# The third expert layer computed for two of its three experts: batches sorted, gathered and scattered by indirect DMA

## Reference

```python
gate_scores = jax.nn.softmax(router_input @ gate_w + gate_b, axis=-1)
top_val, top_idx = jax.lax.top_k(gate_scores, TOP_K)                  # 3 experts, top 2
top_val = top_val / (jnp.sum(top_val, axis=-1, keepdims=True) + 1e-08)
pre = jnp.einsum('bsd,edf->ebsf', h, w1) + b1[:, None, None, :]
act = jnp.stack([jnp.tanh(pre[0]), jax.nn.gelu(pre[1], approximate=False), jax.nn.silu(pre[2])])
expert_out = jnp.einsum('ebsf,efd->ebsd', act, w2) + b2[:, None, None, :]
for i in range(TOP_K):
    j = top_idx[:, 0, i]                                              # by the batch's first row
    moe_out = moe_out + top_val[..., i:i + 1] * expert_out[j, batch_idx]
```

## Time and profile before

| | |
|---|---|
| median of 3 runs | 845.54 us (844.17 to 845.92) |
| profiled execution, its own time | 845.61 us |
| its span, first to last instruction | 843.5 us |
| mean granted clock of PE | 0.988 of full |
| layers 0 and 1 | 0 to 203.2 us of the span |
| layer 2 | 203.2 to 533.2 us |
| layer 3 | 533.2 to 843.5 us |

### The profile page before, as it was taken

The page is one execution under the profiler, slowest core; times in us unless marked ns, Lnnn a source line. Parts: engine busy times, 40 slices in busy tenths (PEclk is TensorE's granted clock), DMA queues, the critical chain, the costliest instruction groups (busy, mean ns, idle before and its releaser), DMA issues.

```text
span 843.5 us, 11203 instructions
## 1 busy us (share of the span) xinstructions
PE 821.4 (97%) x3981; PEld 669.1 (79%) x3981; DVE 385.0 (46%) x850; ACT 289.4 (34%) x541; POOL 247.4 (29%) x272
## 2 busy tenths in 40 slices
PE   4999999998999999999999999999999999999998
PEld 3488777776788888888888888778878888887886
DVE  2567777777322532252225222755454254336522
ACT  5344444444322232233223322234315323432520
POOL 3476677675343210021002100577200220021000
PEclk9699999999999999999999999999999999999999
DMA  8346446432330130013003200433040004002001
GB/s 260 62 114 167 153 155 201 143 131 83 100 100 26 50 111 3 1 62 100 0 0 104 57 0 0 150 99 89 26 137 0 25 14 122 0 25 99 1 1 51
DMA packets 53957, 63.72 MB, mean 76 GB/s; under 512 B 29153, under 2 KB 29409, under 8 KB 53658
## 3 DMA queue, kind: packets, MB, share of 16 engines
q1 hardware_dynamic: 49522, 48.70, 19.7%
q0 software_dynamic: 3888, 14.16, 5.3%
q10 hardware_dynamic: 512, 0.41, 0.2%
HBM read 44.36 MB, written 13.40 MB: 68 GB/s over the span
## 4 chain that ended last, share of the span: by engine, by line
PE 93%; DVE 3%; ACT 1%; DMA 1%; issue 0%; SPq 0%; DVEq 0%; ACTq 0%
PE bank L1456 24%; PE bank L1499 15%; PE bank L1487 15%; PE bank L1441 12%; PE bank L1284 7%; PE bank L1411 5%; PE bank L1229 4%; PE bank L1322 3%; PE bank L1354 1%; PE bank L1334 1%; DMA tap<-in_x_taps_dram 1%; PE bank L1240 1%; PE bank L1276 1%; PE bank L1277 1%; PE bank L1525 0%; PE bank L1519 0%
## 5 line engine op out<-in xcount | busy, mean ns | idle before, releaser
L1089 DVE TENSOR_TENSOR sil<-bank,sil 128x512 f32<-128x512 f32 x56 | 38.7, 691 | 154.3 <-PE bank L1456 154.3
L516 POOL TENSOR_TENSOR tl<-tf,th 128x512 fp32r<-128x512 f32 x16 | 24.0, 1521 | 226.8 <-ACT th L759 226.8
L1456 PE MATMUL bank<-th,wgr 128*128 128x512 f32 x224 | 87.6, 391 | 2.0 <-POOL tl L516 1.8
L1441 PE MATMUL bank<-wdr,hh 128*128 128x512 f32 x224 | 87.4, 390 | 0.0
L1456 PE MATMUL bank<-th,wur 128*128 128x512 f32 x224 | 87.3, 390 | 0.0
L1441 PE MATMUL bank<-wdr,hl 128*128 128x512 f32 x224 | 87.2, 389 | 0.0
L1456 PE MATMUL bank<-tl,wgr 128*128 128x512 f32 x224 | 87.2, 389 | 0.0
L1456 PE MATMUL bank<-tl,wur 128*128 128x512 f32 x224 | 87.2, 389 | 0.0
L1198 DVE TENSOR_TENSOR hl<-sil,hh 128x512 fp32r<-128x512 f32 x48 | 37.1, 772 | 83.7 <-ACT hh L839 83.7
L1499 PE MATMUL bank<-w2h,hh 128*128 128x512 f32 x192 | 75.2, 392 | 0.0
L1499 PE MATMUL bank<-w2h,hl 128*128 128x512 f32 x192 | 74.9, 390 | 0.0
(11 more groups left out here) (251 smaller groups left out, 1866.1 us busy)
## 6 DMA issues: line engine op xcount, KB each, us to landing
xc<-xd SPq DMA_DIRECT2D x32, 256.0 KB, 2.9
xres<-xd SPq DMA_DIRECT2D x8, 1024.0 KB, 5.9
tap<-in_x_taps_dram SPq DMA_DIRECT2D x16, 260.0 KB, 2.8
xin<-in_x_rows_dram SPq DMA_DIRECT2D x16, 256.0 KB, 3.0
xd<-xo SPq DMA_DIRECT2D x16, 256.0 KB, 3.2
xd<-xres SPq DMA_DIRECT2D x4, 1024.0 KB, 4.3
wdr<-in_wd_dram POOLq DMA_DIRECT2D x7, 512.0 KB, 3.7
wgr<-in_wg_dram POOLq DMA_DIRECT2D x7, 512.0 KB, 3.6
```

Of the source, the lines that this page charges most:

```text
L1089: v.tensor_tensor(hf[:, m % 2], p_pre[2 * (m % 2) + 1][:], sil[:, m % 2], ALU.mult).then_inc(s_hf, 1)
L1441: last = mm(p_acc[j][:], h[:, m % HSLOTS, j * P:(j + 1) * P], wdr[:, m], start=(m == 0 and n == 0), stop=(m == MT - 1 and n == 1), skip_gr ...
L1456: last = mm(p_pre[2 * (m % 2) + b][:], w[:, kt, m * P:(m + 1) * P], x[:, kt], start=(kt == 0 and n == 0), stop=(kt == KT - 1 and n == 1))
```

## The change

Layer 3 now works on 16 tiles of 128 rows in a new order of batches. A batch's class is the expert that it doesn't use. Batches are ranked by class and packed in fours: tiles 0 to 13 hold batches of one class and are computed with two experts ("passes" A and B), tiles 14 and 15 hold what is left over and are computed with all three (passes 0, 1 and 2): 34 passes instead of 48 tile-expert pairs. The first ten tiles are filled from groups 0 to 2 while group 3 is still in layer 2; the others are known at pass 16.

- `cond` of layer 3 and the router are moved into layer 2: one group behind, at units 2 to 9 of the next group (`cond3`, `router_sums`, `class_rows`; DVE: `logits`, `route_one`, `route_two`, `classes`), and for the last group into passes 1 to 16. Router logits are now made by DVE. Rows, gates and residual are stored to DRAM (`tsd`, `gsd`, `xd2`).
- Per tile, POOL gathers 128 rows three times by indirect DMA (`gather_t`: rows, `gather_g`: gates, `gather_b`: residual), adds the gated output bias to the residual with six instructions of 128x512 (`bias_rows`), and scatters the result (`scatter`).
- Per tile, PE transposes the gathered rows (`tokens_t`); per pass it does `pre3` (12 matmuls of 512 columns, the rows now stationary, the weights moving), four transposes of the hidden values (`hidden3_t`) and `down3` (12 matmuls), two passes behind. In tiles 0 to 13 the expert's weights are addressed by a register that PE and DVE load from SBUF (`value_load`, two per tile).
- In layer 2, `LAG2` goes from 3 to 2, the hidden slots from 4 to 3 and the banks of gate and up from 4 to 3; the loops over groups are unrolled. The weights of layer 3 are split into halves by POOL during layer 2's last group (`late_split`).

The core of the diff (new functions and the loops that order them):

```diff
+PASSES = [(t, k) for t in range(SINGLE) for k in "AB"] + [(t, k) for t in range(SINGLE, SLOTS) for k in "012"]
+FIRST_PASS = [2 * t if t <= SINGLE else 2 * SINGLE + 3 * (t - SINGLE) for t in range(SLOTS + 1)]
 POOL
+            def gather_t(t):
+                pool.wait_ge(s_idx, 1 if t < EARLY else 2)
+                pool.wait_ge(d_tsd, 16 * (LAST if t < EARLY else GROUPS))
+                if t >= 2:
+                    pool.wait_ge(s_xt, t - 1)
+                nc.gpsimd.indirect_dma_start(xgt[:, t % 2], None, table(tsd, t), row(t)).then_inc(d_gt[t % 2], 16)
...
+            def bias_rows(t):
+                pool.wait_ge(d_b2, 16)
+                pool.wait_ge(d_gb[t % 2], 16 * (t // 2 + 1))
+                pool.wait_ge(d_gg[t % 2], 16 * (t // 2 + 1))
+                for e, g in enumerate((A0, G1, G2)):
+                    if t or e:
+                        pool.wait_ge(ch_xb, 6 * t + 2 * e)
+                    nc.gpsimd.tensor_scalar(tmpb[:], b2c[:, e * D:(e + 1) * D], xgg[:, t % 2, g:g + 1], 1.0, ALU.mult, ALU.mult).then_inc(ch_xb, 1)
+                    pool.wait_ge(ch_xb, 6 * t + 2 * e + 1)
+                    nc.gpsimd.tensor_tensor(xgb[:, t % 2], xgb[:, t % 2], tmpb[:], ALU.add).then_inc(ch_xb, 1)
+            def scatter(t):
+                pool.wait_ge(s_out, t + 1)
+                nc.gpsimd.indirect_dma_start(out.rearrange("t p d -> (t p) d"), row(t), ob[:, t % 2], None).then_inc(d_out[t % 2], 16)
...
+            for t in range(SLOTS):
+                bias_rows(t)
+                if t + 2 < SLOTS:
+                    gather_t(t + 2)
+                    gather_g(t + 2)
+                scatter(t)
+                if t + 2 < SLOTS:
+                    gather_b(t + 2)
 PE
+                pre3(p, at1[p])
+                if p == 0:
+                    down2(LAST, MT - 1)
+                if p + 1 == FIRST_PASS[t + 1] and t + 1 < SLOTS:
+                    tokens_t(t + 1)
+                if p in (2, 4, 6, 8):
+                    cond3(LAST, p // 2 - 1)
...
+                if p >= 1:
+                    hidden3_t(p - 1)
+                if p >= 2:
+                    down3(p - 2, at2[p - 2])
 DVE
+            tokens_lo(0)
+            residual(LAST, s_down, GROUPS * MT)
+            for p, (t, kind) in enumerate(PASSES):
+                if p == FIRST_PASS[t] and t < SINGLE:
+                    dve.wait_ge(s_idx, 1 if t < EARLY else 2)
+                    lacks = [dve.value_load(meta[0:1, i, t:t + 1], min_val=0, max_val=1) for i in range(2)]
+                    v1, v2 = lacks[0] * D, 2 * D - lacks[1] * D
+                b1_add(p, v1, v2)
+                if p + 1 == FIRST_PASS[t + 1] and t + 1 < SLOTS:
+                    tokens_lo(t + 1)
+                if p >= 1:
+                    hidden3_lo(p - 1)
+                activated(p)
+                if p >= 2 and p - 1 == FIRST_PASS[PASSES[p - 2][0] + 1]:
+                    tile_out(PASSES[p - 2][0])
 ACT
+            for p, (t, kind) in enumerate(PASSES):
+                if p + 1 == FIRST_PASS[t + 1] and t + 1 < SLOTS:
+                    tokens_hi(t + 1)
+                if p >= 1:
+                    hidden3_hi(p - 1)
+                functions(p)
```

More of the change, by code:

```diff
@@ L626, in _ @@
+            for i in range(2):
+                pool.wait_ge(d_out[i], 16 * SLOTS // 2)
         @block.scalar
@@ L813, in boundary @@
                 t_hi(c)
[L815 removed]
+            for s in range(GROUPS):
+                c = s - 1
                 for m in range(MT):
@@ new lines, in tokens_t, with rhs @@
+            def tokens_t(t):
+                pe.wait_ge(d_gt[t % 2], 16 * (t // 2 + 1))
+                pe.wait_ge(s_idx, 1)
+                if t >= 1:
+                    pe.wait_ge(s_xtl, t)
+                for k in range(KT):
+                    last = nc.tensor.transpose(bank[3][:, k * P:(k + 1) * P], xgt[:, t % 2, k * P:(k + 1) * P], ident[:])
+                last.then_inc(s_xt, 1)
+            def rhs(tensor, at, dynamic):
+                return tensor[:, bass.ds(at, D)] if dynamic else tensor[:, at:at + D]
@@ new lines, in pre3 @@
+            def pre3(p, at):
+                t, kind = PASSES[p]
+                dynamic = kind in "AB"
+                pe.wait_ge(s_xtl, t + 1)
+                if p == 0:
+                    pe.wait_ge(s_w3, 16)
+                if p == 1:
+                    pe.wait_ge(s_w4, 32)
+                if p < 2:
+                    pe.wait_ge(s_hf, GROUPS * MT - 1 + p)
+                else:
+                    pe.wait_ge(s_s1, p - 1)
+                for k in range(KT):
+                    cols = slice(k * P, (k + 1) * P)
+                    w = (rhs(wda, at + k * D, dynamic), rhs(wda, at + (KT + k) * D, dynamic))
+                    for n, (x, y) in enumerate(parts((xch[:, t % 2, cols], xcl[:, t % 2, cols]), w)):
+                        last = mm(bank[(p + 1) % 2][:], x, y, start=(k == 0 and n == 0), stop=(k == KT - 1 and n == 2))
+                last.then_inc(s_pre, 1)
@@ L1460, in group2 @@
                             integers_t(TILES - 1)
[L1461 removed]
+                        if s == 0 and (m, b) == (2, 0):
                             linear1(TILES - 1)
[L1463 to L1472 removed]
@@ L1563, in _ @@
-            with pe.Fori(0, GROUPS - 1) as r:
-                group3(r)
-            group3(GROUPS - 1, True)
+                    if s >= 1 and 2 <= m < 6:
+                        cond3(c, m - 2)
+                    if s >= 1 and m == 7:
+                        router_sums(c)
+                    if s >= 1 and m == 8:
+                        class_rows(c)
+                    if s == LAST and m == 10:
+                        ranks(0)
+                    if s == LAST and m == 11:
+                        permutation(0)
```

1024 lines of the change are left out of this document (653 added, 371 removed).

## The result

The changed kernel takes 877.49 us (median of 4 runs, 876.1 to 879.2) against 845.47: a ratio of 1.0382 (95% interval 1.036 to 1.0404), slower by 3.8%. The forecast was 856, slower by 1.3%.

What follows compares the result with a forecast made beforehand. PE bounds the kernel before; POOL's gather ring was to bound layer 3. Pass 0 at 546.4, plus 29.3, 5, 45.6 and twelve turns of 19.0, gives 854.3, with 2.1 outside 856 us; range 815 to 893.

Steps and rivals of the forecast that it cites:

- the ring: Layer 3: tile_out, scatter, gather_b, bias_rows, gather_t, then tokens_t ahead of down3; twelve turns of 19.0 us; chance 0.47.
- Layer 2's sum: Layer 2 from 203.2, plus 338.6 us of PE work and 4.6 of waits: pass 0 starts at 546.4.
- PE's saving: Matmuls taken from PE less transposes and router work added: about -87 us, giving 758 were PE never to wait.
- rival 4: Layer 3: PE stays the bound, no closed loop through POOL; 12.9 us a tile, 783 us; chance 0.07.
- e: Layer 3, from tokens_t to the end of tile_out: 5.8 us, bounds 5.2 and 6.9.
- d: POOL's issue of one indirect DMA, three per turn: 1.0 us each, between 0.60 and 1.92.
- B: POOL's bias_rows, six instructions per tile: 7.2 us, bounds 6.4 and 8.4.
- L: Landing of the gathered rows after gather_t's issue: 2.8 us, bounds 2.3 and 3.5.
- the end: After tile_out(12): six passes, the last tile_out and the last scatter, about 4 us; 45.6 us in all.
- The rule on the clock: PE slows after each wait; with a whole tile's work at the lower clock, a turn is 23.1 and the kernel 906.
- P: Time of one tile's turn in layer 3, at least 3d + B + L + e; forecast 19.0 us, break-even 18.1.
- rival 2: Cheap indirect DMAs on POOL: issue 0.6 to 0.7 us, turn 15.9 to 17.9, kernel 819 to 843; chance 0.29.

Runs made afterwards that it cites:

- Experiments 1: Changed kernel with the transposes of gathered rows, and their split on ACT and DVE, moved behind the down product: 826.32 us, ratio 0.9794.
- 3: Changed kernel with POOL issuing the gather of rows for tile t+3 ahead of the scatter of tile t: 796.78 us, ratio 0.9421.
- 2: Changed kernel with POOL issuing the gather of rows ahead of the six bias instructions: 798.18 us, ratio 0.9435.
- Experiment 8: Changed kernel with row gathers three tiles ahead and before the scatter, and the last tile stored by SP as four transfers: 786.27 us, ratio 0.931.
- Experiment 4: Changed kernel with 20 unused matmuls on PE ahead of the transposes of gathered rows, tiles 3 to 14: 852.52 us, ratio 1.0082.
- experiment 6: Changed kernel with all 64 indirect transfers on POOL made plain ones, so rows are not sorted: 852.16 us, ratio 1.0097.
- experiment 5: Changed kernel with one more indirect gather, read by nobody, on POOL behind gather_b in nine tiles: 886.25 us, ratio 1.0479.

## Why the prediction came out as it did

- *The side and the mechanism were right.* Slower, by the ring through POOL, with PE waiting before L1883 for the gather twelve times (forecast 5 to 6 us each, measured 4.3 to 5.2). Experiments 1 and 3 open the ring at two places and 2 takes the bias instructions out of it; in all three PE's waits for the gather fell from 57.5 us to 0.2 or none: this is shown, not argued.
- *Layer 2's sum was right*: pass 0 was forecast at 546.4 and starts at 546.96, the first tile_out at its forecast 575.7 ends at 576.7. The smaller rings of buffers cost nothing visible. The single waits were less well placed: PE waits 2.3 us for the first permutation, where I had 1.0.
- *PE's saving was right*: were PE never to wait, 758, and 783 with the fill and the drain of layer 3 (rival 4). Experiment 8, in which it waits for no gather and the end is short, has 786.27.
- *The step that failed first is a term, e* ("I take 5.8; bounds 5.2 and 6.9"). It measured 7.2, above its own upper bound. I had put only `down3` at the low clock, and part of it. From its first product to what follows it, it took 4.66 us (714.52 to 719.18) for 2.72, still under the 5.2 of my worst case; what went over the bound is the two groups of transposes, which stand behind the same wait (1.63 us from 712.89 to the first down product, for 0.9) and which I had at full clock even in the bound. Experiment 4 gave 2 us of it back.
- *The other terms of the turn*: d 1.0, as taken; B 6.8 for 7.2; L 2.4 for 2.8; the links 0.8 for 0.2, since POOL leaves 0.3 us ahead of an issue. Together 20.1 for 19.0; the sum is nearer than e because B and L, both too high, hid a part of it, and that d, a choice between 0.6 and 1.92 without a row of its own, came out exactly is luck. Over twelve turns the 1.1 is 13; against it stand the 5 us for `logits`, which hardly showed (20.4 to 21.1 in those turns, 20.0 to 20.6 in plain ones later, and two short ones of 18.8 and 19.6). Net 242.3 us from tile_out(0) to tile_out(12), where the forecast had 233: 9.3 of the miss.
- *The second step that failed is the end*: "the last scatter, about 4". The last scatter landed 3.1 us after the last addition's end, and then came 9.1 us that I had nowhere, since the rows of before end with SP. From the end of tile_out(12) to the span's end it was 55.4 for 45.6: 9.8 of the miss, of which 8.3 come after the last addition and 1.5 in the passes before it. With 0.6 at pass 0 and 0.4 up to the first tile these are the 20.1 us between the spans forecast (854.3) and measured (874.4).
- *The rule on the clock.* PE fell to the lower level anew in all twelve turns: the granted clock of the stretch is 0.84, and behind each wait the down products start 0.43 apart. But the clock came back inside each tile's work, after 3 to 10 of the 11 distances, so a turn was 20.1 and not 23.1, the kernel 877 and not 906. Weighing 906 only as an edge of the range was right for the total; that everything right behind the wait is slow, the transposes too, I didn't draw from it. The Trainium skill ("TensorE: Matmul & The Clock Gate", HAM oscillation) tells of a kernel whose work between two DMA waits is shorter than the wait and is throttled anew each time. The trace agrees as to the throttling, though here the work between two waits was some 15.5 us against 4.3 to 5.2 of waiting; so that section's case was not this one, and a whole tile at the low clock didn't follow from it.
- *The break-even.* I wrote that it stands at P = 18.1. Experiment 4 with a turn of 18.2 takes 852.5 and not 847: its end is 9.4 us longer than forecast, and its twelve turns together are 3.5 shorter than 12 x 18.2 + 5.
- *Cheap indirect transfers* (rival 2) didn't turn the sign here: with all of them at a plain issue's 0.54 to 0.59 the kernel takes 852.16 (experiment 6). Its plain turns of 17.1 to 17.6 lie in the rival's range; what keeps it from the rival's 819 to 843 is again the end, three turns of 19.7 to 20.6, and a first `tile_out` 3 us later. With an end as short as SP's store makes it (8.3 less) it would be at about 844, an estimate that no run tests: then the change would be neither won nor lost.
- *Sums that don't come out as written.* Lengthening by 1.52 / 1.29 on half of B's instructions gives 6.9 and not 7.2 (measured 6.8), and that alone would have taken 3.6 us off the forecast. The parts after tile_out(12) add up to 46.5, not 46. The 2.3 for L with which the forecast is 850 is the 2.9 - 0.6 of the earlier trace rows, so a row did show it. And the range from 815 leaves out nothing of rival 2, which starts at 819.

## What to carry to other kernels

When a gather is issued by an engine that also finishes the tile before, write down the ring: which output must be ready before the next input can be asked for, and sum it; if the sum is above the bound engine's work for a tile, all savings on that engine are idle time. Then look for the instruction in that engine's order that could stand behind the gather: here six bias instructions, worth 79 us. And price everything that directly follows a wait of some us at the lower clock, the small transposes too.

## What the runs showed of the hardware that I had not expected

- The span's end follows POOL's last wait by 2.7 us or less in the kernel before, with 27 transfers on POOL's queue, and by 9.1 in the changed one, with 105. Letting SP make the last store took 8.3 us away (877.5 to 869.2).
- How many matmuls after a wait run at 1.2 GHz depends on more than the wait's length. Of the 11 distances in the `down3` behind it, 7 to 10 (once 3) were over 0.33 after 4.3 to 5.2 us in the changed kernel, 4 to 11 after 5.5 to 6.5 in experiment 5, and 3 to 5 (but 8 and 11 in two turns) in experiment 6, after 2.5 to 3.7 and once 5.1. A shorter ring gained, and a longer one lost, other amounts than were taken out or put in (25 for 14, 8.8 for 11.7).
- PE doing 54 us of useless work in its waits (240 x 0.227) made the kernel 25 us faster.
- A single indirect gather in the kernel before landed 6.9 us (at the start) and 5.8 us (late, 4 KB) after POOL began its issue, where the 30 gathers of the other kernel, also of 4 KB, took 2.2 to 2.9 and the changed kernel's gathers of rows 3.2 to 3.7. The first gathers of those two kernels were not slow, so it isn't the program's first as such; the reason stays open.
